# A four-stage graph network on one core: where the third layer's running sums are made, who splits numbers in three, and where TensorE makes its small turns

## The reference

```
logits = einsum('ehd,ehd->eh', Q[dst], K[src]) * scale      # 4 heads
seg_max = segment_max(logits, dst)
e = exp(logits - seg_max[dst]);  w = e / segment_sum(e, dst)[dst]
h_new = segment_sum(V[src] * w[:, :, None], dst)
```

## Time and profile before

| | us |
|---|---|
| median of three executions (4790.32 to 4795.81) | 4792.24 |
| the profiled execution | 4825.84 |
| its span, first to last instruction | 4824.0 |
| PE busy | 3691.8 (77%) |
| DVE busy | 3279.0 (68%) |
| ACT busy | 2725.0 (56%) |
| POOL busy | 2720.9 (56%) |

### The profile page before, as it was taken

The page is one execution under the profiler, slowest core; times in us unless marked ns, Lnnn a source line. Parts: engine busy times, 40 slices in busy tenths (PEclk is TensorE's granted clock), DMA queues, the critical chain, the costliest instruction groups (busy, mean ns, idle before and its releaser), DMA issues. The chain is left out here.

```text
span 4824.0 us, 74391 instructions
## 1 busy us (share of the span) xinstructions
PE 3691.8 (77%) x19148; PEld 2475.9 (51%) x19148; DVE 3279.0 (68%) x8316; ACT 2725.0 (56%) x8902; POOL 2720.9 (56%) x2640
## 2 busy tenths in 40 slices
PE   7958888626289999969577777779999956666565
PEld 2436666425144444559345555555556545555454
DVE  9947999533479999876679999743333446666653
ACT  7936888403178888845246666632333337777522
POOL 5877777775778888507156666430000057777244
PEclk9979999758589999979789999898999968877678
DMA  3023333425233433422456666510000033334334
GB/s 134 23 55 100 94 93 95 66 61 143 58 82 91 92 91 91 62 84 93 132 161 183 181 181 183 131 48 1 14 14 7 12 87 102 102 101 103 36 128 147
DMA packets 278822, 441.38 MB, mean 91 GB/s; under 512 B 114083, under 2 KB 192781, under 8 KB 278157
## 3 DMA queue, kind: packets, MB, share of 16 engines
q0 software_dynamic: 124624, 331.70, 27.2%
q1 hardware_dynamic: 147230, 98.37, 7.2%
q10 hardware_dynamic: 6560, 6.55, 0.4%
HBM read 368.84 MB, written 67.60 MB: 90 GB/s over the span
## 5 line engine op out<-in xcount | busy, mean ns | idle before, releaser
L2501 PE MATMUL PB<-XNT 128*128 128x260 f32 x1760 | 589.3, 474 | 25.7 <-DVE XNT L2475 22.5
L2620 POOL DMA_INDIRECT bigt<-ZTAB,DO x440 | 455.9, 1036 | 168.0 <-issue 114.2
L355 POOL DMA_INDIRECT RECS<-bigt x391 | 460.5, 1178 | 155.9 <-issue 103.3
L1004 POOL DMA_INDIRECT bigt<-HTAB,bigt x440 | 472.1, 1073 | 134.1 <-issue 130.1
L1954 POOL DMA_INDIRECT bigt<-YTAB,bigt x440 | 474.2, 1078 | 119.5 <-issue 118.2
L700 ACT ACTIVATE bigt<-bigt 128x128 f16<-128x128 f16 x1214 | 372.9, 389 | 96.9 <-DVE bigt L673 94.0
L2620 POOL DMA_INDIRECT bigt<-KVTAB,DO x296 | 293.1, 990 | 215.7 <-DMA KVTAB<-bigt 83.9
L2501 PEld LDWEIGHTS PB<-XNT 128*128 128x128 f32 x1760 | 366.0, 230 | 85.7 <-DVE XNT L2383 29.9
L1982 PE MATMUL PB<-bigt 128*128 128x512 f32 x880 | 399.2, 595 | 3.0 <-DVE bigt L2170 3.0
L2052 ACT ACTIVATE bigt<-bigt 128x64 f32<-128x64 f32 x1320 | 327.5, 334 | 83.4 <-DVE bigt L2151 83.4
L2575 ACT ACTIVATE XNT<-bigt 128x65 f32<-128x65 f32 x1472 | 370.0, 334 | 0.0
(11 more groups left out here) (490 smaller groups left out, 9761.9 us busy)
## 6 DMA issues: line engine op xcount, KB each, us to landing
bigt<-YTAB,bigt POOLq DMA_INDIRECT x552
bigt<-SRT SPq DMA_DIRECT2D x56, 128.0 KB, 2.7
OUTS<-bigt SPq DMA_DIRECT2D x56, 128.0 KB, 2.3
SRT<-bigt SPq DMA_DIRECT2D x11, 640.0 KB, 9.8
bigt<-HTAB,bigt POOLq DMA_INDIRECT x440
bigt<-ZTAB,DO POOLq DMA_INDIRECT x440, 2.8
KVTAB<-bigt SPq DMA_DIRECT2D x25, 258.0 KB, 2.3
YTAB<-bigt SPq DMA_DIRECT2D x10, 640.0 KB, 10.5
```

The source lines that it names most:

```text
L355: e.indirect_dma_start(out=RECS, out_offset=bass.IndirectOffsetOnAxis(ap=APOS[:, c:c + 1].bitcast(U32), axis=0), in_=ATTR[:, piece % 2, k, ...
L1004: e.indirect_dma_start(out=Gt[:, g % GB, j, :], out_offset=None, in_=HTAB, in_offset=bass.IndirectOffsetOnAxis(ap=SO[:, g * G + j:g * G + ...
L2501: m = e.matmul(self.PV[n % len(self.PV)], self.OH[:, g % 2, j, :], self.msg[:, g % 2, j, :], start=(k == 0), stop=(k == self.H - 1))
L2620: e.indirect_dma_start(out=dst[:, j, :], out_offset=None, in_=table, in_offset=bass.IndirectOffsetOnAxis(ap=DO[:, g * G + j:g * G + j + 1] ...
```

## The change

In the third layer only (`carry=True`), the running sum is made in PSUM. ACT scales the sum so far (`act_carry`: one scaled copy of 260 columns from PSUM into `AR`, or four of 65 columns at a set's border), and PE adds it to the next half's total by a product with the identity (`total_before`), one step after the total. DVE's `add` is gone there, and ACT copies the finished sum to the accumulator straight from PSUM. The two PSUM buffers of a total come free with that copy.

In both layers all four operations of a split in three stand on DVE, in a row (`split`), and PE's turns of the logits and back stand last in its step where they stood first. In the third layer nearly all lags grow by one step.

```diff
@@ dve
-                    for n in turn(i, L.add, 1, NH):
+                    for n in turn(i, L.add, 1, 0 if self.carry else NH):
                         self.add(e, n)
...
+            def split(self, e, whole, parts, rested, low, s):
+                rest = self.rest[:, 0:self.columns(s)]
+                e.tensor_copy(parts[:, :, 0:4], whole).then_inc(V.up(), 1)
+                e.wait_ge(*V.now())
+                e.tensor_tensor(rest, whole, parts[:, :, 0:4], ALU.subtract).then_inc(rested.sem, 1)
+                e.wait_ge(*rested.at(s))
+                e.tensor_copy(parts[:, :, 4:8], rest).then_inc(V.up(), 1)
+                e.wait_ge(*V.now())
+                e.tensor_tensor(parts[:, :, 8:12], rest, parts[:, :, 4:8], ALU.subtract).then_inc(low.sem, 1)
@@ total
-                    e.wait_ge(*self.added.at(n - len(self.PV)))
+                    e.wait_ge(*(self.kept if self.carry else self.added).at(n - len(self.PV)))
...
-                                 start=(k == 0), stop=(k == self.H - 1))
-                m.then_inc(self.summed.sem, 1)
+                                 start=(k == 0), stop=(k == self.H - 1 and not self.carry))
+                m.then_inc(self.multiplied.sem, 1)
+            def total_before(self, e, n):
+                if n:
+                    e.wait_ge(*self.carried.at(n - 1))
...
+                e.matmul(self.PV[n % len(self.PV)], ident[:, :], self.AR[:, n % 3, :], start=False,
+                         stop=True).then_inc(self.summed.sem, 1)
+            def act_carry(self, e, n):
+                pv, nxt = self.PV[n % len(self.PV)], self.AR[:, (n + 1) % 3, :]
+                s, r = divmod(n + 1, self.R)
+                e.wait_ge(*self.summed.at(n))
+                if r:
+                    m = e.activation(nxt, pv, ACT.Copy, scale=self.same[:, n + 1:n + 2])
+                else:
+                    e.wait_ge(*self.shrink.at(s))
+                    for h in range(4):
+                        d = slice(65 * h, 65 * h + 65)
+                        m = e.activation(nxt[:, d], pv[:, d], ACT.Copy, scale=self.fs[:, s % 2, h:h + 1])
+                m.then_inc(self.carried.sem, 1)
@@ pe, in a step
+                    for n in turn(i, L.total + 1, 1, NH if self.carry else 0):
+                        self.total_before(e, n)
                     for n in turn(i, L.total, 1, NH):
                         self.total(e, n)
@@ act, in a step
                     for n in turn(i, L.add, 1, NH):
+                        if self.carry and n < NH - 1:
+                            self.act_carry(e, n)
                         tile = tile_of(e, "act", TTD, n)
-                        e.wait_ge(*self.added.at(n))
+                        e.wait_ge(*(self.summed if self.carry else self.added).at(n))
@@ l2_gnn
-            ... Lags(oh=1, turn=3, oht=4, side=SIDE, tl=16, scan=16, back=17, split=17, node=18, top=19,
-                                              edge=20, shift=20, msg=21, total=23, add=24), (3, 7))
+            ... Lags(oh=1, turn=3, oht=4, side=SIDE, tl=16, scan=17, back=17, split=18, node=19, top=20,
+                                              edge=21, shift=21, msg=22, total=24, add=25), (3, 7), True)
```

More of the change, by code:

```diff
@@ L2365, in dve @@
                                         ALU.is_equal).then_inc(self.onehot.sem, 1)
[L2366 to L2375, removed]
                     for g in turn(i, L.msg, 2, NG):
@@ L2507, in pe @@
                 e.wait_ge(*self.prepared.last)
[L2508 to L2520 removed]
+                for i in range(NH + L.total + 2):
                     for s in turn(i, L.node, R, S):
@@ L2550, in pe @@
                                          for j in range(n % 2 * self.H, n % 2 * self.H + self.H)])
+                    for s in turn(i, L.tl, R, S):
+                        n, c0 = self.columns(s), s * C
+                        if s:
+                            e.wait_ge(*self.rested.at(s - 1))
+                        e.matmul(self.TK[0:4 * n], self.DKB[:, c0:c0 + n].rearrange("p c h -> p (c h)"), self.step, start=True, stop=True)
+                        e.wait_ge(*self.logged.at(s))
+                        e.transpose(self.TL[0:4 * n], self.LOG[:, s % 2, 0:n].rearrange("p c h -> p (c h)"),
+                                    ident[:, :]).then_inc(self.log_turned.sem, 1)
+                    for s in turn(i, L.back, R, S):
+                        n = self.columns(s) * 4
+                        e.wait_ge(*self.masked.at(s))
+                        e.transpose(self.BK[:, 0:n], self.Fm[0:n], ident[0:n, 0:n]).then_inc(self.log_back.sem, 1)
             def act(self, e, values, v_in):
@@ L2585, in act @@
-                    for s in turn(i, L.split, R, S):
-                        n = self.columns(s)
-                        e.wait_ge(*self.log_back.at(s))
-                        if s >= 2:
-                            e.wait_ge(*self.node_max.at(s - 2))
-                        e.activation(self.PC[:, s % 2, 0:n, 0:4], self.BK[:, 0:4 * n].rearrange("p (c h) -> p c h", h=4),
-                                     ACT.Copy).then_inc(self.high.sem, 1)
-                        e.wait_ge(*self.rested.at(s))
-                        e.activation(self.PC[:, s % 2, 0:n, 4:8], self.rest[:, 0:n], ACT.Copy).then_inc(self.middle.sem, 1)
@@ L2601, in act @@
+                        e.activation(self.ACC[:, bass.ds(tile, 1), :], row.unsqueeze(1), ACT.Copy).then_inc(self.kept.sem, 1)
+                    for s in turn(i, L.top, R, S):
                         e.wait_ge(*self.drop.at(s))
-                        if s >= 2:
+                        if s >= 2 and not self.carry:
                             e.wait_ge(*self.added.at(R * (s - 2)))
+                        elif s > 2:
+                            e.wait_ge(*self.carried.at(R * (s - 2) - 1))
```

59 lines of the change are left out of this document (21 added, 38 removed).

## The result

The changed kernel takes 4839.26 us, median of four executions (4836.69 to 4842.23), beside 4791.61 of the kernel before on the same chip: 1.0098 times as long, 95% interval 1.0081 to 1.0116. The profiled execution took 4842.23 us, its span is 4840.4.

A forecast was written before the change was run, and what follows sets the result against it. It took DVE to pace the third layer and POOL's gathers the fourth. Terms +36 + 4 - 3 = +37 on the median 4792.2 gave 4829 us, 0.8% slower; range 4768 to 4872.

The forecast's parts named there:

- The gather loop: Third layer: chain through scaled copy, message, gathers, key product, `maximum` and exponential paces a set at 24.8 us, before 23.39.
- The wait that was to show it: Third layer: DVE's key product waits for gathers once a set, mid-stage, over 1 us.
- Two signs: Third layer: ACT waits 2 us or more for DVE's subtracted maximum in phase 5; DVE's busy share falls to about 80%.
- POOL's two terms: Third layer: POOL starts 0.27 us after the message's end, then issues three more gathers, 3.75 us in all.
- +1.4 us a set, +36: Third layer: the longer chain costs 1.4 us in each of 26 sets, +36 us; range +29 to +52.
- ends and fourth layer: Longer lags and slower drained steps cost +4 us; fourth layer's DVE waits for ACT's rounding go for about one set, -3.
- The chain over the turn back: Third layer, rival that gathers stay covered: turn back paces at 23.3 us a set, about 4791 us; chance 0.15.
- Only ACT and PE hand over, 21.7: Third layer rival: only scaled copy, product and message pace, 21.7 us a set, 4749 us; chance 0.10.
- The clock falls on the loop: Third layer rival: PE at 1.2 GHz at each phase 7 restart, +1.6 us a set, +40, 4869 us; chance 0.13.
- The casts hold POOL: Fourth layer rival: three more DVE copies from SBUF a set delay POOL's gathers, +19, 4848 us; chance 0.05.
- The splits: On DVE: each rounding copy taken as 0.23 us, a whole split of four dependent operations as 0.9 us.

The follow-up runs named there:

- read9: Changed kernel with the third layer's key product one step later (READ 9, SUM 10, query side 7): 4752.8 us, 0.9951 of the kernel before.
- oh2: Changed kernel with the third layer's one-hot build one step later (lag 2 for 1): 4797.6 us, 1.0023 of the kernel before.
- splits_c: Kernel before with both three-part splits on DVE alone; sums on DVE, turns first, lags as before: 4801.2 us, 1.0007 of the kernel before.
- carryfirst: Changed kernel with turns first in both layers and the third layer's lags as before; carry and splits kept: 4733.7 us, 0.9890 of the kernel before.
- nocarry: Changed kernel with the third layer's running sum back on DVE; lags, splits and turn order as changed: 4819.0 us, 1.0068 of the kernel before.

## Why the prediction was right, and where its numbers were not

The forecast was +37 us (4829); +47.7 was measured. The gather loop's links, as forecast and as medians over 22 sets of the trace after:

| from, to | forecast | measured |
|---|---|---|
| scaled copy (phase 7), one-hot copy | 1.25 | 1.32 |
| one-hot copy, message | 0.91 | 0.92 |
| message, its end | 2.54 | 2.53 |
| message's end, first gather | 0.27 | 0.74 |
| first, fourth gather | 3.75 | 4.65 |
| fourth gather, key product | 4.16 | 3.89 |
| key product, end of the subtraction | 7.53 | 7.51 |
| exponential, up to the message | 0.55 | 0.32 |
| message, scaled copy of phase 6 | 2.45 | 2.45 |
| scaled copy, product, scaled copy | 1.36 | 1.25 |
| sum | 24.8 | 25.6 |

*The gather loop is the mechanism.* Six of the ten links are within 0.12 us, and read9 and oh2 moved the time by changing two different parts of it. The wait that was to show it, once a set at the key product of phase 4 and over 1 us, is there (2.42 in the set above). Two signs came weaker than I had put them: ACT waits for DVE's subtracted maximum 33.0 us in 19 waits, 1.7 each and never over 2.0, where I had 2 or more, and DVE's share fell to 76%, not 80.

*Mis-sized: POOL's two terms.* POOL's start was taken from a wait for DVE's message (0.27); for ACT's message, the one that ends last here, it is 0.74. And the first of the four gathers takes 1.84 instead of 0.95, since DVE's one-hot build runs under it. The term "+1.4 us a set, +36" was 25.7 - 23.5 = 2.2 by medians, and with the uneven sets 2.66, so 64 us from first to last turn: outside the +29 to +52 that I gave the term. That range was itself too wide for what I had put into it: it counts four DVE copies at their ends, and only the two of the split behind `maximum` stand in the chain.

*Mis-sized the other way: ends and fourth layer.* I had +4 and -3. Behind the third layer's turns the two traces differ by -3.4, -5.8 and -8.2. The -3.4 is where my +4 should have been. The fourth layer's -5.8 has the sign of the term and twice its size, but its 28 turns took 594.1 us in splits_c and 590.6 in carryfirst, with the same code, so some 3.5 us are chance or chip. The -8.2 behind the last turn is not explained by the change: that piece took 308.3 us in the trace before, but 304.0 in splits_c and 300.1 in the kernel after. The third layer's term was 28 us too small and the rest 18 us too large; that the total came within 11 us of the measured one was in good part luck.

*The chain over the turn back was priced too long.* I gave 23.3 as the set's length if the gathers were covered. read9 gives their cover back and runs at 22.46, so the price was too high. Whether that chain paces read9 is not shown: PE waits only 7.5 of 500 us there for DVE's split, and mostly ACT and PE wait for each other (56.2 us, and 29.3 the other way).

*Only ACT and PE hand over, 21.7.* It did not come with the change, but carryfirst is near this case: 21.1 by the median, with ACT and PE at 424 and 439 of 500 us and waits of DVE for rows at about a third (29.6 for 82.4).

*The clock falls on the loop.* The low level does appear, but in phase 5, behind PE's wait for DVE's split: in 13 of 22 sets a total there takes 1.67 to 1.94 us (1.94 at 2801.63, behind a wait of 2.45; compare). ACT waits there for DVE's subtraction anyway (1.54 us at 2804.34), and the sets with it and those without have the same median length, 25.7 us, so it costs the chain nothing. In phase 7 the totals take 1.04. (In the rival's own price, 0.4 + 0.9 + 0.4 is 1.7, not 1.6.)

*The casts hold POOL.* Wrong in size. In the trace after, four gathers of the third layer started under a cast from SBUF of 0.2 us, and none took over 0.95. In nocarry one did take longer, by 0.06 us:

```profile
2459.84 0.21 DVE L2395 CAST bigt<-bigt 128x64 bf16<-128x64 f32 x1
2459.87 1.01 POOL L2634 DMA_INDIRECT X<-KVTAB,DO  x1 [0.30 <-issue]
```

The fourth layer's turns became shorter, where +19 had been the rival's price. That something of DVE's lengthens gathers was right; it is other instructions, below.

*The splits.* The four operations behind `maximum` took 0.21, 0.26, 0.20 and 0.23 us by the medians, 0.91 from the first to the next instruction, as assumed (those that read PSUM first 0.24, 0.23, 0.20 and 0.23); the scaled copy 0.48 and 0.46 where I took 0.43, inside the bounds.

Open: how much of the loss is the turns' place and how much the lags. That the lost step of cover carries most of it is shown by read9, with the turns left last; a time of the kernel with turns first and later lags exists only for the chips with unnamed waits. Open too: what separates read9 (22.46) from carryfirst (21.60).

## What to carry to other kernels

When work is taken off the busiest engine and put into a hand-over between two others, write down the loop from one set to the same place in the next, with every lag that the move shifts. Here the lag of the messages went from 21 to 22 and took one of five steps of cover from the gathers. A ring keeps its cover if the instruction that reads it moves as far as the one that frees it: moving the read one step later as well (three numbers) gave back 1.5% and made the change a gain. With the old lags and the turns first, the same carry and splits gave -1.1% where the change had +1.0%. In such a loop the wake-up of an engine and what runs beside it count nearly in full: in oh2 1.5 of the 2.0 us taken out of a set came off its length.

## What the hardware showed that I had not expected

*Which DVE instructions lengthen a gather.* In the trace after 52 of the third layer's 440 gathers take over 1.2 us, two a set, 1.6 on average; nearly all others 0.94 to 0.96. All but two of the long ones start while DVE runs its one-hot build or a message, instructions with two operands from SBUF, and end 0.81 to 0.83 us after it: the build of 2788.00 ends at 2789.21 and its gather at 2790.03, the message of 2804.82 at 2805.51 and its gather at 2806.33, the build in oh2 at 2790.06 and its gather at 2790.88. Under reductions of the same 1.22 us (one operand, 62 gathers between 2500 and 3050 us) and under key products (one operand in PSUM, 94 gathers) no gather took over 0.96. Not lengthened either were gathers that started within 0.03 us of the build's or the message's start, or in its last 0.1 us. The Trainium skill's page "SBUF — State Buffer", section "Who interferes with whom", says that an instruction of VectorE with two inputs in SBUF contends with one of GpSimd that reads SBUF; these gathers read their row numbers there, and on this the trace agrees (1.84 us in place of 0.95).

*POOL wakes later behind ACT than behind DVE*: 0.74 us from the end of ACT's last message copy to the first gather's start (41 times in the trace after, 2500 to 3060 us), 0.27 behind DVE's message (21 times). The 0.74 contains ACT's own end as the trace models it; what makes the difference was not tried.
